# Reordered first stages and cross-attention order, with filler products in TensorE's waits: one core, a chain of twelve small layers

## The chip, the cores and the metric

The kernel runs as one program on one NeuronCore of a Trainium2 chip. Its five instruction streams are TensorE (PE, with its weight loads shown apart as PEld), VectorE (DVE), ScalarE (ACT), GpSimd (POOL) and SyncE (SP), which issues nearly all DMA transfers. The metric is the device time of one execution in microseconds (us); lower is better.

## The reference, cut to what matters

The input x is a sequence of 128 rows of 128 numbers. It passes through twelve layers (four levels, each a cross-attention, a self-attention and a feed-forward part). A context of 2048 rows of 128 numbers is attended to by the cross layers `l0x`, `l1x`, `l2x` and `l3x`. Everything is float32, and each layer needs the whole result of the layer before it.

```python
# l0x (level 0): similarity of each context row and each query, both ways, then one product
S      = sim(norm(x), ctx)                    # [128, 2048]
c2q    = softmax(S, over context) @ ctx       # [128, 128]
q2c    = softmax(max(S, over context)) @ norm(x)      # one row of 128
x      = x + concat(xn, c2q, xn * c2q, xn * q2c) @ W_qv + b_qv
# l0a: linear attention with rotary positions on q and k, projection, residual
# l0f: 16-head attention, router, top 2 of 8 experts, residual
# l1x: 16-head cross-attention over the 2048 context rows, with a mask
# l1a: linear attention;  l1f: four hard-routed trees of 256 leaves (q, k, v, f)
# l2x: 16-head cross-attention over the context;  l2a, l2f: attention, experts
# l3x: 16 heads of width 64 over the context;  l3a, l3f: attention, gated experts
```

The rows' order of dependence is strict: no layer can start its main work before the one before it ends. What does not depend on x (the keys of `l1x`, products of two weight matrices, the relative-distance bias `d.1` to `d.3`, a row that marks masked context rows) can be put anywhere before its use.

## The kernel before

The program is written out by hand: every layer is a function that gives each engine a list of instructions, and each engine works through its list in order. `Steps` is a counting semaphore with names: `plan` fixes the order of the names, `now` marks the instruction that completes one, and `wait_ge(..., at(name))` makes another engine wait for it. So an instruction that waits holds up everything behind it on its own engine.

`l0x` has the start of the program. SP issues twelve loads in one order, the context transposed (`ctxT`, 1 MB) fifth, then `rows` (all row vectors), `ctx`, `w_a` (all weights of level 0 and 1) and `const`. PE runs products of ones as filler, transposes the normalised x, makes four score products of 512 context rows each against `tA`, and DVE takes their maxima. ACT makes the exponentials in four quarters, PE turns each quarter (four transposes, `turn`), DVE or ACT copies it to SBUF and PE weighs the context with it (`weigh`). Only after that comes the short softmax over the row maxima (`l0x.t`, `l0x.row`, `l0x.rowexp`, `l0x.batt`, `l0x.bar`). Then the reciprocal of the sums is spread over a 128x128 tile, turned by a product with the identity (`l0x.rd`), copied, multiplied in, and four products with `w_l0x` and an addition make `l0x.x`.

`l0a` works on x with its norm applied late. Between its own steps it has the keys of `l1x` in four parts of 512 (`keys_tensor` on PE, `keys_scalar` on ACT for the high half, `keys_vector` on DVE for the low half), the mask (`mask.any`, `mask`), and two of three steps of the distance bias. q and k are rotated one after the other by `rotate`, five DVE instructions each. `l0f` starts with `biases_tensor` and its self-attention.

When the last low part is made, SP stacks the keys (`stack_keys`): twelve transfers from SBUF to SBUF and three single-row copies, on the one queue. The first GpSimd instruction of `l1x` waits for all of them, and the norm of `l1x` is behind it.

`cross` is the function of `l1x` and `l2x`. For each of 16 heads it needs the maximum of the scores over the context (`peak`: two score products of 512 on PE, one DVE reduction of 128x1024), and then scores again in the other layout (`score`: one product of 512, into one of three banks), an exponential on ACT and the weighing (`weigh`: four narrow products of 256). The main loop is made of runs: four times peak, score, score; then `turn(q + 1)`, which brings the maxima of the next four heads into the queries (`place` on DVE follows); then eight times `weigh`. DVE takes the sums of four heads at `take`.

`l1f` is the tree stage: gathers of leaves by GpSimd, whose landing PE and DVE wait for. `keep(n, bank)` issues n products of the identity with itself, 128 columns in bfloat16, `keep_wide` the same with 512 columns; neither result is read. `l3x` is the last cross layer; there PE waits for the maxima, DVE and ACT for the first two heads.

## Time and profile before

| | |
|---|---|
| median of 3 runs | 502.78 us (501.64 to 502.9) |
| the profiled execution, its own time | 507.33 us |
| its span, first to last instruction | 505.5 us |
| PE busy | 469.7 us (93%), 4058 instructions |
| DVE busy | 326.9 us (65%) |
| ACT busy | 247.1 us (49%) |
| POOL busy | 69.1 us (14%) |
| mean granted TensorE clock | 0.986 |
| end of `l0x`, `l0a`, `l0f` in the span | 28.07, 38.33, 64.57 us |

The busy shares are averages over stages with different limits, and PE's contains the filler products; a busy PE is not by itself the bound. The stages follow one another strictly, so the end of a stage is the time at which DVE has written the new x, and a stage's length is the distance of two such ends.

### The profile page before, as it was taken

The numbers are of one execution on the slowest core, as the hardware profiler recorded it, in microseconds if no ns is written. First come the engines' busy times: TensorE is split into PE (matmuls) and PEld (weight loads), VectorE is DVE, ScalarE is ACT, GpSimd is POOL, SyncE is SP. The second block draws the span as 40 slices with busy tenths as digits, with TensorE's granted clock in tenths as the row PEclk, the third lists the DMA queues.
The fourth block names the chain that finished last, engine by engine and source line by source line (L and its number), as shares of the span: only waits on it lengthen the run. The fifth ranks groups of instructions, "written<-read, shape, count | busy, mean of one in ns | idle before, by whom it ended". The sixth has DMA issues, their size and how long they took to land.

```text
span 505.5 us, 10078 instructions
## 1 busy us (share of the span) xinstructions
PE 469.7 (93%) x4058; PEld 382.7 (76%) x4058; DVE 326.9 (65%) x802; ACT 247.1 (49%) x490; POOL 69.1 (14%) x152
## 2 busy tenths in 40 slices
PE   8989998999877898999998899889999999999897
PEld 6858885565564786856657789779989989989797
DVE  4676679886645935898526663476777877755544
ACT  6324546777302434666744246356557656522131
POOL 1230134000016120200005015400000000001000
PEclk9999999999998988999999999989999999999999
DMA  7908302900188432100009100000000000029000
GB/s 258 409 6 180 74 1 60 206 10 1 44 315 337 181 109 106 43 1 1 1 10 406 46 1 2 0 1 0 1 1 2 1 1 1 1 80 412 8 1 6
DMA packets 9070, 42.05 MB, mean 83 GB/s; under 512 B 2287, under 2 KB 4919, under 8 KB 6327
## 3 DMA queue, kind: packets, MB, share of 16 engines
q1 hardware_dynamic: 7297, 32.73, 19.9%
q0 software_dynamic: 1728, 8.68, 4.6%
q8 instruction: 32, 0.52, 0.4%
q14 instruction: 13, 0.11, 0.1%
HBM read 34.72 MB, written 0.08 MB: 69 GB/s over the span
## 4 chain that ended last, share of the span: by engine, by line
PE 66%; DVE 18%; issue 6%; ACT 4%; DMA 3%; POOL 2%; POOLq 0%; DVEq 0%; ACTq 0%
PE banks L286 59%; PE banks L289 7%; DVE peaks L1627 4%; DMA region<-in_tree_f,leaf_no 2%; ACT probs L2773 1%; DMA region<-in_tree_q,leaf_no 1%; DVE region L1910 1%; DVE small L2691 1%; DVE nmax L661 1%; ACT probs L689 1%; DVE probs L1910 1%; DVE weights_lo L2701 1%; DVE xnT L409 1%; POOL mv L396 1%; ACT region L1714 1%
## 5 line engine op out<-in xcount | busy, mean ns | idle before, releaser
L1627 DVE TENSOR_REDUCE peaks<-banks 128x1 f32<-128x1024 f32 x56 | 66.2, 1219 | 3.6 <-PE banks L286 2.6
L286 PE MATMUL banks<-identb 128*128 128x128 bf16 x826 | 57.7, 221 | 0.6 <-DVE mv L381 0.6
L286 PEld LDWEIGHTS banks<-identb 128*128 128x128 bf16 x826 | 52.1, 100 | 3.9 <-DVE mv L381 0.9
L2691 DVE TENSOR_REDUCE small<-banks 128x1 f32<-128x1024 f32 x32 | 39.1, 1222 | 21.4 <-PE banks L286 21.1
L2773 ACT ACTIVATE probs<-banks,nmax,rooted 128x1024 f32<-128x1024 f32 x32 | 38.5, 1205 | 24.2 <-DVE nmax L2695 23.6
L2782 ACT CAST weights_hi<-banks 128x512 fp32r<-128x512 f32 x64 | 35.1, 590 | 26.1 <-PE banks L289 23.5
L289 PE MATMUL banks<-p_first,probs 128*128 128x128 f32 x320 | 45.0, 279 | 1.9 <-ACT probs L689 1.1
L2701 DVE TENSOR_TENSOR weights_lo<-banks,weights_hi 128x512 fp32r<-128x512 f32 x64 | 41.5, 683 | 7.6 <-ACT weights_hi L2782 7.6
L1714 ACT ACTIVATE region<-banks,seen 128x512 f32<-128x512 f32 x64 | 37.9, 702 | 12.1 <-PE banks L286 12.0
L289 PEld LDWEIGHTS banks<-p_first,probs 128*128 128x128 f32 x320 | 37.0, 142 | 8.5 <-ACT probs L689 2.5
L1714 ACT ACTIVATE region<-banks 128x512 f32<-128x512 f32 x64 | 33.3, 606 | 16.4 <-PE banks L286 16.0
L396 POOL TENSOR_TENSOR mv<-mv,half 128x1 f32<-128x1 f32 x12 | 6.7, 555 | 236.0 <-DVE mv L390 148.2
L286 PE MATMUL banks<-weights_hi,rows_hi 128*128 128x256 f32 x128 | 37.3, 291 | 0.7 <-DVE weights_lo L2701 0.7
L286 PE MATMUL banks<-weights_lo,rows_hi 128*128 128x256 f32 x128 | 36.2, 283 | 0.0
L286 PE MATMUL banks<-weights_hi,rows_lo 128*128 128x256 f32 x128 | 36.0, 281 | 0.0
L286 PE MATMUL banks<-xnT,region 128*128 128x128 f32 x266 | 33.9, 277 | 0.9 <-DVE xnT L409 0.8
L286 PEld LDWEIGHTS banks<-xnT,region 128*128 128x128 f32 x266 | 31.4, 191 | 1.9 <-DVE xnT L409 1.8
L286 PE MATMUL banks<-region,values 128*32 128x256 f32 x512 | 31.7, 382 | 0.0
L286 PE MATMUL banks<-ctx_hi,query_r 128*128 128x512 f32 x64 | 27.4, 428 | 3.8 <-ACT probs L2773 3.8
L286 PE MATMUL banks<-ctx_hi,query_lo 128*128 128x512 f32 x64 | 25.6, 400 | 0.0
L286 PE MATMUL banks<-ctx_lo,query_r 128*128 128x512 f32 x64 | 25.3, 396 | 0.0
L286 PEld LDWEIGHTS banks<-weights_hi,rows_hi 128*128 128x128 f32 x128 | 24.3, 190 | 0.9 <-DVE weights_lo L2701 0.9
(516 smaller groups left out, 924.3 us busy)
## 6 DMA issues: line engine op xcount, KB each, us to landing
region<-in_w_l2f SPq DMA_DIRECT2D x1, 4096.0 KB, 15.5
region<-in_w_l3f SPq DMA_DIRECT2D x1, 4096.0 KB, 13.4
region<-in_w_b SPq DMA_DIRECT2D x1, 3076.0 KB, 13.6
values<-in_ctx SPq DMA_DIRECT2D x2, 1024.0 KB, 7.6
region<-in_w_l0f SPq DMA_DIRECT2D x1, 2048.0 KB, 21.7
keys_l1x<-shared SPq DMA_DIRECT2D x8, 256.0 KB, 4.0
keys_l2x<-probsT SPq DMA_DIRECT2D x8, 256.0 KB, 4.9
region<-in_w_l3d SPq DMA_DIRECT2D x1, 2048.0 KB, 17.1
```

Source lines behind the costliest of these rows:

```text
L286: return nc.tensor.matmul(o, lhsT, rhs, start=start, stop=stop)
L289: return nc.tensor.transpose(o, i, ident[0:n, 0:n])
L396: nc.gpsimd.tensor_tensor(mv[:, 3:4], mv[:, 2:3], half[:, 0:1], ALU.pow).then_inc(G.sem, G.now(tag + ".rstd"))
L409: nc.vector.tensor_copy(dst[0:n, :], ps[0:n, bank, 0:P]).then_inc(V.sem, V.now(tag + ".T"))
L661: m = nc.vector.tensor_reduce(m4, s, AX.X, ALU.max, negate=True)
L1627: nc.vector.tensor_reduce(peaks[:, h // 4 % 2, i:i + 1], ps[:, 2 * a:2 * a + 2, :], AX.XY, ALU.max, negate=True).then_inc(VM.sem, VM.now(( ...
L1714: nc.scalar.activation(weighed[:, u % HELD * BANK:(u % HELD + 1) * BANK], ps[:, score_bank(u), :], ACT.Exp, scale=seen[:, 0:1] if masked e ...
L1910: m = nc.vector.tensor_tensor_reduce(w, x, w, 1.0, 0.0, ALU.mult, ALU.add, h[:, j:j + 1])
L2691: return nc.vector.tensor_reduce(small[:, half:half + 1], ps[:, 2 * half:2 * half + 2, :], AX.XY, ALU.max)
L2701: nc.vector.tensor_tensor(sides(g, c, weights_lo), turned(g, c).rearrange("p (a b) -> p a b", a=4), sides(g, c, weights_hi).bitcast(F32), ...
L2773: nc.scalar.activation(probs[:, g % 2, o:o + 2 * BANK], ps[:, 2 * half:2 * half + 2, :].rearrange("p a b -> p (a b)"), ACT.Exp, bias=nmax[ ...
L2782: nc.scalar.copy(sides(g, c, weights_hi), turned(g, c).rearrange("p (a b) -> p a b", a=4)).then_inc(A.sem, A.now((tag, "e", g, c)))
```

## The change

In `l0x`: the first memset is that of the ones, and only it is waited for. The loads are in another order and in parts: `ctxT` in four, `rows` in three, `w_a` in two, `const` in two, the mask as a 128x16 tile. The sums of the small row softmax are worked on between the quarters of the large one, the division by the sums is moved into the last instruction, and `l0x.rd` with its spreading, product and copy is gone. Of the two products with `center`, one moves to `l1x`; `d.1` moves to `l0f`. GpSimd prepares its constants while the loads land.

In `l0a`: q and k are rotated together in one set of instructions of twice the width; only two parts of the keys are left, both halves of each are written by ACT (`key_scalar`), and the differences are made by GpSimd in `l0f` (`low_gpsimd`); `biases_tensor` moves here, between the product `l0a.kv` and `l0a.c`.

In `l0f`: the other two parts of the keys, the four differences on GpSimd, `d.1` and `d.2`. In `l1x`: `d.3` and the other product with `center`, ahead of the stage. The three single-row copies of `stack_keys` become four early loads from DRAM.

In `cross`: score goes ahead of peak in each group of three, and `turn` goes into the middle of the eight `weigh`. In `l1f`, `keep` has 60 more products of 128 columns; in `l3x`, 7 and 8 products of 512 columns are put in two waits.

```diff
         def norm_vector(...):
             ...tensor_scalar(mv[:, 2:3], mv[:, 1:2], eps, ...).then_inc(V.sem, V.now(tag + ".var"))
+            if between is not None:
+                between()
             dve.wait_ge(G.sem, G.at(tag + ".rstd"))
@@ sp @@
-            load("ctxT", ctxT[:, :], dram["ctxT"])
-            load("rows", rows_t[:, :], dram["rows"].partition_broadcast(P))
-            load("ctx", values, dram["ctx"])
-            load("w_a", tiles["w_a"][:, :], dram["w_a"])
-            load("const", tiles["const"][:, :], dram["const"])
+            load("mask_by_row", mask_t[:, :], dram["mask"].rearrange("o (p c) -> (o p) c", c=16))
+            for b in QUARTERS:
+                load(f"ctxT{b}", ctxT[:, b * BANK:(b + 1) * BANK], dram["ctxT"][:, b * BANK:(b + 1) * BANK])
+            load_part("rows0", rows_t, dram["rows"], 0, 2, ROWS)
+            load_part("w_a0", tiles["w_a"], dram["w_a"], 0, 5, W_A)
+            load("ctx", values, dram["ctx"])
+            load_part("const0", tiles["const"], dram["const"], 0, 10, CONST)
+            load_part("rows1", rows_t, dram["rows"], 2, 7, ROWS)
+            load_part("w_a", tiles["w_a"], dram["w_a"], 5, len(W_A), W_A)
+            load_part("const", tiles["const"], dram["const"], 10, len(CONST), CONST)
+            load_part("rows", rows_t, dram["rows"], 7, len(ROWS), ROWS)
@@ l0x, pe @@
+                turn(0)
+                turn(1)
+                pe.wait_ge(V.sem, V.at("mask"))
+                product(1, 0, xnT, True, False)
+                weigh(0)
+                pe.wait_ge(V.sem, V.at("l0x.row"))
+                mm(batt, tC[0:1, :], one[0:1, 0:1]).then_inc(T.sem, T.now("l0x.batt"))
+                turn(2)
+                weigh(1)
+                pe.wait_ge(V.sem, V.at("l0x.batt"))
+                mm(bar, xn[:, :], s[:, 8:9]).then_inc(T.sem, T.now("l0x.bar"))
+                turn(3)
+                weigh(2)
+                pe.wait_ge(V.sem, V.at("l0x.f"))
+                product(1, 3, tF, False, True).then_inc(T.sem, T.now("l0x.y0"))
+                weigh(3)
+                fill(6)
+                pe.wait_ge(V.sem, V.at("l0x.prod"))
+                product(2, 2, tE, True, False)
+                pe.wait_ge(V.sem, V.at("l0x.d"))
+                product(2, 1, tD, False, True).then_inc(T.sem, T.now("l0x.y"))
@@ l0x, dve: maxima @@
+                loaded(dve, "rows0")
+                vl(dve, nc.vector.tensor_tensor_reduce(tC[:, :], xn[:, :], at["w1"], ...))
+                nc.vector.tensor_tensor(s[:, 1:2], s[:, 0:1], at["b_sim"], ALU.add)
+                for b in QUARTERS:
+                    dve.wait_ge(T.sem, T.at((tag, "s", b)))
+                    m = nc.vector.tensor_reduce(small[:, b:b + 1], ps[:, b, :], AX.X, ALU.max)
...
+                nc.vector.scalar_tensor_tensor(xs[:, 1 - x_at[tag], :], ps[:, 2, 0:P], s[:, 10:11], xb[:, :], ALU.mult,
+                                               ALU.add).then_inc(V.sem, V.now("l0x.x"))
@@ l0a, pe @@
+                keys_tensor(pe, "l1x", at["w_l1x_k"], 0, 2)
+                keys_tensor(pe, "l1x", at["w_l1x_k"], 1, 3)
+                keep(4, 6)
+                pe.wait_ge(V.sem, V.at("l0a.qk"))
+                mm(ps[:, 1, 0:P], rotated[:, P:2 * P], tC[:, :]).then_inc(T.sem, T.now("l0a.kv"))
+                tr(ps[:, 5, 0:P], rotated[:, 0:P]).then_inc(T.sem, T.now("l0a.q.turned"))
+                pe.wait_ge(G.sem, G.at("wide"))
+                biases_tensor(4)
@@ l0f, pool @@
+                pool.wait_ge(V.sem, V.at("l0f.xn"))
+                for b in range(NB):
+                    low_gpsimd(pool, "l1x", b, shared)
@@ cross, pe @@
                     for i in range(4):
+                        score(RUN * (d + 1) + 2 * i)
                         peak(4 * d + LEAD + i)
-                        score(RUN * (d + 1) + 2 * i)
                         score(RUN * (d + 1) + 2 * i + 1)
...
-                    if c == 0 and q + 1 < QUADS:
-                        turn(q + 1)
                     for u in range(RUN * d, RUN * (d + 1)):
+                        if u == RUN * d + RUN // 2 and c == 0 and q + 1 < QUADS:
+                            turn(q + 1)
                         weigh(u)
@@ l1f, pe: keep() @@
-                keep(8, 0)
+                keep(30, 0)
                 pe.wait_ge(A.sem, A.at("l3x.vo"))
                 tree_tensor(pe, "q")
                 tree_tensor(pe, "k")
+                keep(6, 2)
...
                 first_units(pe, "v")
+                keep(16, 2)
                 pe.wait_ge(A.sem, A.at("l1f.p"))
...
                 tree_tensor(pe, "v")
+                keep(8, 2)
...
-                keep(6, 2)
+                keep(10, 2)
                 turn_tensor(pe, "l1f.y", tB[:, :], "l1f.y", 7)
-                keep(6, 2)
+                keep(10, 2)
@@ l3x, pe @@
                 against_context(1, (0, 1), 1)
+                keep_wide(7, 4)
                 pe.wait_ge(G.sem, G.at("l3x.rows"))
...
+                    if g == 0:
+                        keep_wide(8, 6)
```

## Rows read from the trace of the kernel before

**Rows 1.** Page, part 4: shares of the chain that ended last.

```profile
PE 66%; DVE 18%; issue 6%; ACT 4%; DMA 3%; POOL 2%; POOLq 0%; DVEq 0%; ACTq 0%
```

**Rows 2.** Stretches: start and end, length, busy time (count) by engine, clock, DMA.

```profile
28.10:38.40 10.30, 9.13 (x57) 5.44 (x56) 8.25 (x30) 2.75 (x4) 1.78 (x8) 1.00 0.01 2
82.00:137.00 55.00, 52.12 (x419) 31.78 (x420) 42.99 (x82) 37.91 (x64) 3.45 (x9) 1.00 0.35 69
```

**Rows 3.** DMA issues: KB, us from issue to landing.

```profile
ctxT<-in_ctxT SPq DMA_DIRECT2D x1, 1024.0 KB, 5.5
```

**Rows 4.** Timeline of `l0x`: start, duration, instruction, idle before and releaser.

```profile
2.42 0.43 SPq L312 DMA_DIRECT2D ctxT<-in_ctxT  x1
...
8.04 3.65 PE L286 MATMUL banks<-ctxT,tA 128*128 128x512 f32 x8
...
12.65 0.15 DVE L551 TENSOR_SCALAR nmax<-small 128x1 f32<-128x1 f32 x1
...
16.25 0.63 PE L289 MATMUL banks<-p_first,probs 128*128 128x128 f32 x4
...
16.71 1.06 PE L286 MATMUL banks<-probsT,values 128*128 128x128 f32 x8
...
21.14 0.28 DVE L954 TENSOR_REDUCE small<-banks 1x1 f32<-1x128 f32 x1 [1.95 <-PE banks L289]
...
27.78 0.29 DVE L446 TENSOR_TENSOR xs<-banks,xb 128x128 f32<-128x128 f32 x1 [0.88 <-PE banks L286]
```

**Rows 5.** Timeline of `l0a`, the same columns.

```profile
31.57 0.34 DVE L1090 SCALAR_TENSOR_TENSOR tG<-banks,mv,p_rows 128x128 f32<-128x128 f32 x1
...
34.20 0.49 PE L286 MATMUL banks<-tC,tB 128*128 128x128 f32 x2 [0.42 <-DVE tB L1097]
...
36.46 0.38 PE L286 MATMUL banks<-tE,tD 128*128 128x128 f32 x2
...
37.65 1.14 PE L286 MATMUL banks<-own_bias,sbq 64*128 64x4 f32 x8
...
38.05 0.28 DVE L446 TENSOR_TENSOR xs<-banks,xb 128x128 f32<-128x128 f32 x1
```

**Rows 6.** Timeline: first and last group of 15 key transfers; one GpSimd difference.

```profile
38.16 1.23 SPq L312 DMA_DIRECT2D keys_l1x<-shared  x2
...
52.27 1.25 SPq L312 DMA_DIRECT2D keys_l1x<-keys_l1x  x1
...
72.11 1.28 POOL L1339 TENSOR_TENSOR keysT<-keysT,probsT 128x512 f32<-128x512 f32 x1 [0.86 <-ACT keysT L1333]
```

**Rows 7.** Timeline of `l1x`: two peaks' maxima, then weigh, peak, exponentials.

```profile
102.12 2.35 DVE L1627 TENSOR_REDUCE peaks<-banks 128x1 f32<-128x1024 f32 x2
...
112.47 1.93 PE L286 MATMUL banks<-region,values 128*32 128x256 f32 x32
114.33 0.73 PE L286 MATMUL banks<-keys_l1x,query_r 105*128 105x512 f32 x2
...
115.33 4.74 ACT L1714 ACTIVATE region<-banks,seen 128x512 f32<-128x512 f32 x8 [1.62 <-PE banks L286]
```

**Rows 8.** Stretches of `l1f` and `l3x`, columns as in Rows 2.

```profile
178.00:180.00 2.00, 2.00 (x17) 1.86 (x15) 0.84 (x3) 0.00 (x0) 0.00 (x0) 0.50 0.00 0
...
334.00:336.00 2.00, 2.00 (x11) 1.77 (x10) 0.98 (x1) 1.02 (x4) 0.00 (x0) 0.69 0.00 0
336.00:338.00 2.00, 2.00 (x8) 1.71 (x7) 1.59 (x3) 1.05 (x2) 0.00 (x0) 0.50 0.00 0
```

**Rows 9.** Timeline of PE in `l1f` and `l3x`, columns as in Rows 4.

```profile
156.20 5.73 PE L286 MATMUL banks<-routes,identb 128*128 128x512 bf16 x18 [2.03 <-DMA region<-in_tree_q,leaf_no]
163.36 4.06 PE L286 MATMUL banks<-p_first,region 128*128 128x128 f32 x34 [1.44 <-DVE small L1917]
...
179.46 1.18 PE L286 MATMUL banks<-xnT,shared 128*128 128x128 f32 x4
...
333.29 0.50 PE L286 MATMUL banks<-ctx_hi,query_r 128*128 128x512 f32 x1 [2.05 <-ACT probs L2773]
```

More of the change, by code:

```diff
@@ L250, in build @@
         loads = {n: sem("loaded_" + n) for n in
-                 ("x", "first", "w_k2", "const", "cols", "rows", "w_a", "ctxT", "ctx", "mask", "w_l0f", "l0f_b2", "node",
+                 ("x", "first", "w_k2", "const0", "const", "cols", "rows0", "rows1", "rows", "w_a0", "w_a", "ctxT0", "ctxT1",
+                  "ctxT2", "ctxT3", "ctx", "mask_by_row", "w_l0f", "l0f_b2", "node",
                   *("leaf1_" + t for t in "qkvf"), *("leaf0_" + t for t in "qkvf"),
@@ L312, in load, with load_part @@
             nc.sync.dma_start(dst, src, allow_slow_non_contiguous=scattered).then_inc(loads[name], 16)
+        def load_part(name, tile, source, first, last, pack):
+            at_ = [sum(w for _, w in pack[:i]) for i in range(len(pack) + 1)]
+            c = slice(at_[first], at_[last])
+            if source is dram["rows"]:
+                load(name, tile[:, c], source[c].partition_broadcast(P))
+            else:
+                load(name, tile[:, c], source[:, c])
         def loaded(eng, name):
-            eng.wait_ge(loads[name], {"node": 64, "keys_l1x": 15 * 16, "keys_l2x": 12 * 16}.get(name, 16))
+            eng.wait_ge(loads[name], {"node": 64, "keys_l1x": 16 * 16, "keys_l2x": 12 * 16}.get(name, 16))
         @on("sp")
@@ L869, in l0x @@
-            V.plan("l0x.q", "center")
-            G.plan("prelude", "pairs", "wide")
+            norm_plan(tag)
+            T.plan("l0x.xn.turned")
+            V.plan("l0x.q", "l0x.xn.T", "hidden", "mask.min", "center")
+            G.plan("prelude", "wide", "pairs")
             A.plan(*(("shown", t) for t in range(4)))
-            ctx_plan(tag, 1)
-            V.plan("l0x.t")
-            T.plan("l0x.row")
-            V.plan("l0x.rowmax")
-            A.plan("l0x.rowexp")
-            V.plan("l0x.row")
@@ new lines, in product @@
+                def product(bank, i, f, start, stop):
+                    return mm(ps[:, bank, 0:P], f[:, :], at["w_l0x"][:, i * P:(i + 1) * P], start, stop)
+                pe.wait_ge(G.sem, G.at("one"))
+                fill(30)
+                loaded(pe, "first")
+                turn_tensor(pe, tag + ".xn", xn[:, :], tag + ".xn")
+                fill(8)
+                pe.wait_ge(V.sem, V.at("l0x.q"))
+                for b in QUARTERS:
+                    loaded(pe, f"ctxT{b}")
+                    mm(ps[:, b, :], tA[:, :], ctxT[:, b * BANK:(b + 1) * BANK]).then_inc(T.sem, T.now((tag, "s", b)))
@@ new lines, in _ @@
+                loaded(pe, "w_a0")
+                pe.wait_ge(V.sem, V.at("center"))
+                centred_tensor(pe, 0, 4)
+                mm(ps[:, 7, 400:401], one[:, :], masked_t[:, 16:17]).then_inc(T.sem, T.now("mask.any"))
+                fill(12)
+                pe.wait_ge(V.sem, V.at("l0x.t"))
+                tr(row, s[:, 2:3]).then_inc(T.sem, T.now("l0x.row"))
+                fill(4)
+                turn(0)
+                turn(1)
+                pe.wait_ge(V.sem, V.at("mask"))
@@ L1134, in _ @@
                 loaded(act, "cols")
-                for b in range(NB):
-                    keys_scalar(act, "l1x", at["l1x_bk"], b, 2 + b % 2, shared)
+                key_scalar(act, "l1x", 0, 2, shared, at["l1x_bk"])
+                act.wait_ge(T.sem, T.at("l0a.q.turned"))
+                nc.scalar.copy(tE[:, :], ps[:, 5, 0:P]).then_inc(A.sem, A.now("l0a.q.T"))
+                key_scalar(act, "l1x", 1, 3, shared, at["l1x_bk"])
             @on("pool")
@@ L1163, in _ @@
             def _(pe):
-                pe.wait_ge(G.sem, G.at("wide"))
-                biases_tensor(1)
-                pe.wait_ge(G.sem, G.at("prelude"))
-                keep(14, 0)
+                for b in (2, 3):
+                    pe.wait_ge(A.sem, A.at(("l1x", "k", b - 2)))
+                    keys_tensor(pe, "l1x", at["w_l1x_k"], b, b)
                 pe.wait_ge(V.sem, V.at("l0f.var"))
-                keep(10, 0)
+                keep(6, 0)
                 start_tensor(pe, tag)
```

578 lines of the change are left out of this document (225 added, 353 removed).

## The prediction

> **What bounds the kernel now.** I read the chain of waits first: two thirds of it are PE, a fifth DVE [rows 1], but PE's share contains filler and products that wait in PE's list for DVE. A mean over the span says little here, so I then went through the timeline stage by stage, asking what released each step. The twelve layers are strictly serial: whatever a stage loses is lost, and whatever is off its chain costs nothing.
>
> In `l0x` the score products start at 8.04, when `ctxT` has landed (issued 2.42, 5.5 later, so 7.9), and the maxima are ready at 12.80 (12.65 + 0.15). From there to the new x at 28.07 (27.78 + 0.29) are 15.27 us [rows 3, 4]. The row softmax comes after the whole weighing: its first DVE step is at 21.14 after 1.95 of idle [rows 4]. In `l0a` DVE is busy 8.25 of 10.30 us with things of which the keys, mask and distance are not the stage's own [rows 2]. In the crosses no engine is full (DVE 42.99, ACT 37.91 of 55.00 [rows 2]), so each run is a chain of hand-overs.
>
> **`l0x`: the start.** `ctxT` in quarters lets the first score start when a quarter is there. The quarter is the fifth load as the whole was; I estimate 5.7, between the issue at 2.42 and the whole's 7.9. Four scores take 3.65, so they end at 9.4 rather than 11.7. But DVE now waits for `rows0` ahead of the maxima, and that load is behind all of `ctxT`: not before 7.9, about 8.1, plus 0.6 for the two instructions on it. Four maxima at 0.7 and the two small steps (3.1 together) give 11.7 to 11.9 for the maxima instead of 12.80: I take 11.7, a gain of 1.1. Bounds: nothing if `rows0` is at 9, and 2.3 if `rows0` is no wait.
>
> **`l0x`: after the maxima.** Counted from the maxima (0). ACT: two exponentials of 0.7, the row's exponential 0.5, two more: last at 3.3. PE: a turn is 0.63, a weighing 0.95 (8 passes in 1.06, overlapped) [rows 4]. Turns 0 and 1 end at 2.15; the mask's wait behind DVE's first copy holds PE to 2.5; product 0.25, weighing 0 to 3.7, row product 0.35, turn 2 to 4.7, weighing 1 to 5.6, next row product to 5.9, turn 3 to 6.5, weighing 2 to 7.4, product, weighing 3 to 8.7. Then a DVE product 0.3, another copy behind it, two pairs of passes and the closing instruction: 10.1. Against 15.27 that is 5.2 less. The removed parts are the row softmax behind the weighing (21.14 to about 23.7) and the spreading, product and copies of the reciprocal. `l0x` together gains 6.3; bounds 4.5 (each of six new hand-overs 0.3 worse) and 8.
>
> What leaves `l0x` is hidden later: one product with `center` and `d.3` ahead of `l1x` stand where `keep(16)` stood; DVE's copy of `d.3` (0.41) is in the 0.7 in which it waits for GpSimd's root; `d.1` and `d.2` stand in `l0f`'s waits, where I count 0.1 lost. Without that cover they would cost about 1.5.
>
> **`l0a`.** Both rotations take 31.57 to 34.20, 2.63. At twice the width in one set I work out 1.8: the fixed part of five instructions is saved, the elements are not. The mask and distance steps ahead and between are gone, and so is the fourth key product, behind which the product of 36.46 stood: that came 2.26 after 34.20, with a key difference on DVE between [rows 5]. New chain from x: turned x at 1.0, v and q,k to 1.9, rotated 3.7, `kv` 3.75, turn of q, and then `biases_tensor`, eight small passes, which took 1.14 at 37.65 with nothing waiting, now ahead of `l0a.c`: it starts at 5.3 instead of 4.6. From there the old tail, 38.33 - 36.46 = 1.87. So 7.2 instead of 10.26 [rows 5]: gain 3.1, bounds 2.2 (if ACT's two writes of part 0 hold its copy of q) and 3.7 (if the eight passes are hidden).
>
> **`l0f` and the keys.** The last GpSimd difference decides when SP can stack. GpSimd starts after `l0f.xn`, about 30.6 on the new time; four of 1.28 [rows 6] end at 35.8. The 15 transfers took 38.16 to 53.52; without three of them 11.5, so the last is issued at 47.3 and lands some 4.4 later, 51.7. GpSimd must have them before the norm of `l1x`, at 28.9 + 26.2 + 0.8 = 55.9. The queue has 4 us to spare; I cost it at nothing. The DVE time freed was counted in `l0a`. `l0f` keeps its 26.2, plus the 0.1.
>
> **The crosses.** After weighing ends PE does a peak first (114.33, 0.73 with its tail), and ACT begins only at 115.33 after 1.62 idle; then eight exponentials take 4.74 [rows 7]. Score first brings ACT's start about 0.45 forward. What can take it back is DVE: two maxima take 2.35 [rows 7], a peak may be issued only when the one two before is taken, and `turn` half a weighing later makes `place` 0.95 later. With those limits: the run after a `turn` stays about 6.3 (DVE ends last, no gain), the other falls from 6.67 to about 6.0, also because `turn` no longer waits at the head of the weighing. That is 0.7 to 0.9 per four heads, and 0.3 to 0.45 in the last two runs, where DVE has no peaks. Over three and a half such groups: 2.2 in `l1x`, 1.8 in `l2x` (shorter exponentials, so DVE binds more). Together 4.0; bounds 0 and 5.4 (12 runs by 0.45).
>
> **The filler.** In `l1f` the clock was granted at 0.50, which is 1.2 GHz, in 178 to 180: (1 - 0.5) x 2 = 1.0 us of lost PE time, and the node products there took 1.18 for four passes [rows 8, 9], where others take 0.6. They are on the chain to the last gather. With 24 more fillers just before I take the clock as held: 1.0 gained. Against it, fillers that outlast their wait by 0.1 each, in four places: 0.4. Net 0.6, bounds -1.0 and 1.3. The 22 extra at 154 fill an idle of 2.03 and let the 18 wide ones run at full clock, but nothing waits for these: they end at 160 instead of 161.9. In `l3x` the wait of 2.05 before 333.29 was followed by 0.69 and 0.50 of the clock: 0.62 + 1.0 = 1.6 us lost [rows 8, 9]. Eight wide products at 0.22 are 1.76 and fit in 2.05, seven are 1.54 in the earlier wait of 1.7. I take 1.4, bounds 0 and 1.6.
>
> Sum: 6.3 + 3.1 - 0.1 + 4.0 + 0.6 + 1.4 = 15.3. The profiled execution took 507.33 (span 505.5), so 492.0 in its terms; the median lies 4.55 below it, 502.78 - 15.3 = 487.5.
>
> **The clock and a rule against the change.** The wides now ending at 160 leave PE idle until 163.36: 3.3 us, where 1.44 did no harm and 2.03 (ahead of 156.20) was followed by the half clock [rows 9]. The Trainium skill, "TensorE: Matmul & The Clock Gate", "HAM oscillation", says that waits of PE which are long enough drop the clock and that the work after them starts slow. The longer gap of this change fits that rule; the idle of 2.05 in rows 9 agrees with it. By this the 34 passes of 4.06 after 163.36 would run at half for a while, some 2 us later; DVE sets the chain there and has about 1 us of room, so the loss is up to 1.0: the lower bound above.
>
> The Trainium skill, "DMA: Bandwidth & Descriptors", "Measured", wants transfers of 1 MiB and more, against quarters of `ctxT`. No row here shows a quarter; by the rule the last one and `rows0` come late, which is the rival of the loads below.
>
> **Rivals.** (a) The crosses give nothing: score in front holds the peak back behind ACT's bank, and DVE, 42.99 of 55.00, starves. For it: DVE is the fullest there. Against: DVE idles anyway at every `take`. Gain 15.3 - 4.0 = 11.3, time 491.5; if each of 12 runs loses 0.23, the length of one score, 494. (b) Loads late: the parts land slower than the whole, `rows0` at 10 and `ctx` behind it. Costs 2 to 3 in `l0x`: 490. (c) The fillers hold no clock and the tree's gap drops it: 15.3 - 2.0 - 1.0, time 490.5. (d) Slower than before: the queue of keys. If GpSimd's differences or SP's transfers end late, the norm of `l1x` waits behind them. It begins to cost when the keys land after 55.9, 4.2 later than worked out, and turns the sign only when they land 15.3 + 4.2 = 19.5 later, at 71. That takes 13 us more than the 11.5 for twelve transfers; nothing in rows 6 hints at it. 503 to 506. (e) The change does nothing: the new order only moves the waits. The 5.2 of removed chain in `l0x` speaks against it.
>
> **How the numbers follow.** Main case with its bounds 0.58; (a) 0.17; (b) 0.11; (c) 0.08; (d) 0.03; (e) 0.03. The prediction is the main case, 487.5. All terms at their best give 8 + 3.7 + 5.4 + 1.3 + 1.6 = 20.0, all at their worst 4.5 + 2.2 + 0 - 1.0 + 0 - 0.1 = 5.6, or 482.8 and 497.2. I leave out the ends where all terms would have to agree: 483 to 495, which holds (a) to (c). A difference of 0.3% (1.5 us) is about what a measurement of this kernel can tell from none: faster by more 0.95, within it 0.02, slower by more 0.03.
>
> **What would show it.** `l0x` should end near 21.8, `l0a` 7.2 later, `l0f` 26.2 after that. ACT's first exponential of a run should come 0.6 after the weighing, not 1.0. The windows of 2 us around the end of tree v, and in `l3x` after the second head's exponentials, should show clock 1.00. Keys should be stacked before GpSimd's first instruction in `l1x`. I am wrong if `l0x` ends after 24, if the `cross` runs keep 6.3 and 6.7, or if the clock falls in the tree's new gap and DVE waits for PE there.

## The result and the profile after

| | before | changed |
|---|---|---|
| median, us (lowest to highest) | 502.84 (501.64 to 506.43), 4 runs | 494.69 (493.65 to 496.35), 4 runs |
| ratio of the changed kernel to before | | 0.9835 (95%: 0.9804 to 0.9866) |
| profiled execution, own time / span | 507.33 / 505.5 | 495.39 / 493.6 |
| mean granted clock in it | 0.986 | 0.993 |

The change gains 8.15 us by the medians, where 15.3 was forecast: 494.69 against 487.5. A ratio, here and below, is taken against the kernel before as timed beside that run, whose medians lie between 502.8 and 504.7; so medians of different experiments compare only roughly. By stages (each ends with DVE's write of the new x; us):

| stage | before | before, second profile | changed | gain forecast |
|---|---|---|---|---|
| `l0x` | 28.07 | 28.49 | 24.56 | 6.3 |
| `l0a` | 10.26 | 10.25 | 7.02 | 3.1 |
| `l0f` | 26.24 | 26.24 | 26.25 | -0.1 |
| `l1x` | 71.24 | 71.27 | 70.15 | 2.2 |
| `l1f` | 55.04 | 50.62 | 52.34 | 0.6 |
| `l2x` | 66.00 | 66.18 | 65.19 | 1.8 |
| `l3x` | 139.72 | 137.86 | 138.05 | 1.4 |

The other five stages agree within 0.02 in all three. The column in the middle is an experiment further down; `l1f` and `l3x` cannot be read without it. The stages of the two first profiles differ by 13.0, their spans by only 11.9: from the last write of x to the end of the span, where the output is stored, the changed kernel's profile took 3.1 and the first of before 1.95. All others took 1.9 to 2.0 there, so the 1.1 belongs to that one execution.

The changed kernel's `l0x` in the timeline (start, duration, engine, instruction, idle before it and releaser); its rows answer to [rows 4]:

```profile
4.49 0.43 SPq L315 DMA_DIRECT2D p_rows<-in_rows  x1
4.96 0.43 SPq L315 DMA_DIRECT2D p_w_a<-in_w_a  x1
5.44 0.43 SPq L315 DMA_DIRECT2D values<-in_ctx  x1
5.89 2.82 PE L292 MATMUL banks<-ctxT,tA 128*128 128x512 f32 x6
5.91 1.44 SPq L315 DMA_DIRECT2D p_const<-in_const  x1
7.39 1.51 SPq L315 DMA_DIRECT2D p_rows<-in_rows  x1
...
9.07 1.12 PE L292 MATMUL banks<-ctxT,tA 128*128 128x512 f32 x2 [0.36 <-DMA ctxT<-in_ctxT]
...
10.97 0.29 DVE L850 CUSTOM_DVE_ANT_0 tC<-xn,p_rows 128x128 f32<-128x128 f32 x1 [4.77 <-DMA p_rows<-in_rows]
...
11.38 2.48 DVE L856 TENSOR_REDUCE small<-banks 128x1 f32<-128x512 f32 x4
...
12.24 1.55 PE L292 MATMUL banks<-p_w_a,center 128*128 128x384 f32 x2 [2.05 <-DMA p_w_a<-in_w_a]
...
14.09 0.15 DVE L859 TENSOR_SCALAR nmax<-small 128x1 f32<-128x1 f32 x1
...
24.21 0.35 DVE L895 SCALAR_TENSOR_TENSOR xs<-banks,small,xb 128x128 f32<-128x128 f32 x1 [0.60 <-PE banks L292]
```

The first three scores follow one another without a wait, but DVE stands for 4.77 us before its first use of `rows0`, and then takes four maxima in a row that could have gone between the scores. The maximum is ready at 14.24, which is 1.4 later than before, not 1.1 earlier. From there to the end it is 10.32 instead of 15.27; that half of the change works. PE idles meanwhile, from 10.19 to 12.24, and then the granted clock falls to 0.50, which is 1.2 instead of 2.4 GHz (the same kernel by stretches, columns as in [rows 2]):

```profile
10.00:12.00 2.00, 0.19 (x1) 0.00 (x0) 0.99 (x5) 0.00 (x0) 0.00 (x0) 1.00 1.03 420
12.00:14.00 2.00, 1.76 (x6) 1.15 (x7) 1.97 (x5) 0.00 (x0) 0.00 (x0) 0.59 0.97 404
14.00:16.00 2.00, 2.00 (x21) 1.94 (x19) 0.55 (x4) 1.57 (x5) 0.10 (x1) 0.55 1.07 433
```

`l0a`, against [rows 5]: the eight small passes start at 28.91, and `l0a.c` (the product of `tE` and `tD`) follows them.

```profile
28.91 0.29 DVE L1042 SCALAR_TENSOR_TENSOR tD<-banks,p_const 128x128 f32<-128x128 f32 x1 [0.58 <-PE banks L292]
28.91 1.14 PE L292 MATMUL banks<-own_bias,sbq 64*128 64x4 f32 x8
29.02 0.27 ACT L1053 COPY tE<-banks 128x128 f32<-128x128 f32 x1 [0.30 <-PE banks L295]
29.91 0.47 PE L292 MATMUL banks<-tE,tD 128*128 128x128 f32 x2
...
31.29 0.29 DVE L471 TENSOR_TENSOR xs<-banks,xb 128x128 f32<-128x128 f32 x1 [0.58 <-PE banks L292]
```

A pair of runs in `l1x`, against [rows 7]: in the first run (98.44) `turn` is inside the weighing, which is thus split, and ACT starts 2.62 after the weighing's start; in the second 2.39. Before it was 2.86 (115.33 - 112.47).

```profile
98.44 1.28 PE L292 MATMUL banks<-region,values 128*32 128x256 f32 x19
99.55 1.05 PE L292 MATMUL banks<-region,values 128*32 128x256 f32 x13
...
101.06 4.86 ACT L1635 ACTIVATE region<-banks,seen 128x512 f32<-128x512 f32 x8 [1.54 <-PE banks L292]
104.94 1.94 PE L292 MATMUL banks<-region,values 128*32 128x256 f32 x32
107.33 4.28 ACT L1635 ACTIVATE region<-banks,seen 128x512 f32<-128x512 f32 x7 [1.42 <-PE banks L292]
```

`l1f` around the new gap behind the wide fillers (they end at 152.29, PE goes on at 154.78), by stretches:

```profile
153.00:155.00 2.00, 0.22 (x2) 0.22 (x3) 1.59 (x4) 1.19 (x5) 1.20 (x2) 1.00 1.04 422
155.00:157.00 2.00, 1.83 (x13) 1.74 (x13) 1.98 (x18) 1.25 (x5) 0.00 (x0) 0.68 1.01 424
157.00:159.00 2.00, 2.00 (x11) 2.00 (x11) 1.93 (x18) 0.00 (x0) 0.00 (x0) 0.50 1.00 405
```

The low stretch did come right behind that gap, as was feared. Those of [rows 8] are gone, but they were gone in the second profile of before too.

### The profile page after: what moved, and what is told of

Same layout as the page of the kernel before. It is cut to its first block, busy times and chain, and to the rows that moved or that the text cites. A ratio compares the mean times of both kernels' runs of the same rounds, so it can differ in the third digit from the quotient of the medians.

```text
span 493.6 us, 9957 instructions
## 1 busy us (share of the span) xinstructions
PE 463.6 (94%) x3994; PEld 375.7 (76%) x3994; DVE 317.9 (64%) x789; ACT 249.8 (51%) x494; POOL 73.9 (15%) x156
## 4 chain that ended last, share of the span: by engine, by line
PE 67%; DVE 12%; issue 7%; DMA 5%; ACT 4%; POOL 3%; SPq 1%; POOLq 0%; DVEq 0%; ACTq 0%
PE banks L292 60%; PE banks L295 7%; DMA region<-in_tree_v,leaf_no 2%; DVE peaks L1546 2%; DMA region<-in_tree_f,leaf_no 2%; DMA p_w_a<-in_w_a 1%; ACT probs L2700 1%; DVE small L2618 1%; POOL region L1748 1%; POOL mv L421 1%; DVE nmax L557 1%; SPq L315 1%; ACT probs L585 1%; DVE weights_lo L2628 1%; DVE xnT L434 1%
## 5 line engine op out<-in xcount | busy, mean ns | idle before, releaser
L1635 ACT ACTIVATE region<-banks,seen 128x512 f32<-128x512 f32 x64 | 38.3, 700 | 10.5 <-PE banks L292 10.3
L292 PEld LDWEIGHTS banks<-region,values 128*32 128x32 f32 x512 | 16.2, 109 | 13.4 <-ACT region L1635 2.9
```

Source lines behind the costliest of these rows:

```text
L292: return nc.tensor.matmul(o, lhsT, rhs, start=start, stop=stop)
L1635: nc.scalar.activation(weighed[:, u % HELD * BANK:(u % HELD + 1) * BANK], ps[:, score_bank(u), :], ACT.Exp, scale=seen[:, 0:1] if masked e ...
```

## The experiments

Twelve runs: eleven kernels, and the kernel before once more. Unless a text says otherwise, "the changed kernel" is their base.

**rows_first**

```diff
+            load_part("rows0", rows_t, dram["rows"], 0, 2, ROWS)
             for b in QUARTERS:
                 load(f"ctxT{b}", ...)
-            load_part("rows0", rows_t, dram["rows"], 0, 2, ROWS)
```

> The changed kernel with one issue moved: the load of the first two row vectors (`rows0`) is issued ahead of the four quarters of `ctxT`, not behind them. Theory: DVE waits at the head of the maxima only for this load; in the changed kernel it landed at 10.97 though the fourth score ended at about 10.2 and the first at 6.7. With it first it lands by 7 to 8, DVE takes the maxima as the scores come, and the last quarter, one issue (0.43) later, sets them: scores end at 10.6, maxima ready at about 11.7 to 12.0 instead of 14.24, l0x 2.2 to 2.5 us shorter, and nothing after it changes. Rival: the queue gives the transfers a fixed share, so the broadcast row load delays the quarters by as much as it took, the last quarter lands at 10 or later, and l0x gains 1 us or less.

Median 491.55, ratio 0.9785 (0.9748 to 0.9821), which overlaps the changed kernel's 0.9804 to 0.9866 a little. `l0x` 21.95, 2.61 shorter, of which 0.5 is the clock, which did not fall here; `l0a`, `l0f` and both crosses as in the changed kernel. Timeline:

```profile
6.12 0.29 DVE L850 CUSTOM_DVE_ANT_0 tC<-xn,p_rows 128x128 f32<-128x128 f32 x1
...
8.00 0.69 DVE L856 TENSOR_REDUCE small<-banks 128x1 f32<-128x512 f32 x1 [1.38 <-PE banks L292]
...
9.87 1.13 PE L292 MATMUL banks<-ctxT,tA 128*128 128x512 f32 x2 [0.19 <-DMA ctxT<-in_ctxT]
...
11.03 0.69 DVE L856 TENSOR_REDUCE small<-banks 128x1 f32<-128x512 f32 x1 [0.63 <-PE banks L292]
...
11.95 0.15 DVE L859 TENSOR_SCALAR nmax<-small 128x1 f32<-128x1 f32 x1
```

The maxima now follow the scores; the last quarter sets the end. Maximum at 12.10, end 9.85 later. What the two orders do to the queue is seen in the DMA view (0 to 16 us in 40 slices, GB/s; then KB and us from issue to landing), first of the changed kernel:

```profile
GB/s 0 0 0 0 78 113 156 61 19 175 261 256 302 271 271 379 328 225 129 32 26 42 128 196 225 352 437 420 461 430 410 438 387 416 368 432 423 436 428 447
ctxT<-in_ctxT SPq DMA_DIRECT2D x4, 256.0 KB, 3.7
p_rows<-in_rows SPq DMA_DIRECT2D x1, 64.5 KB, 6.5
```

and of rows_first:

```profile
GB/s 0 0 0 0 108 99 116 74 31 41 53 116 86 268 375 353 369 353 266 302 215 102 230 333 420 461 471 410 410 426 384 404 387 405 415 452 411 457 291 382
ctxT<-in_ctxT SPq DMA_DIRECT2D x4, 256.0 KB, 4.0
p_rows<-in_rows SPq DMA_DIRECT2D x1, 64.5 KB, 3.5
```

With `rows0` in the middle there is a trough of 26 to 42 GB/s from 7.6 to 8.8, and SP's issues there take 1.44 and 1.51 instead of 0.43; with it in front the low rates (31 to 116) come from 2.8 to 5.2, and no single issue takes over 0.74. The price is that the first score starts at 6.86 instead of 5.89; it costs nothing at the end, because the last quarter sets that.

**dot_after**

```diff
-                loaded(dve, "rows0")
-                ...tensor_tensor_reduce(tC, xn, at["w1"], ...); tensor_tensor(s[:, 1:2], ...)
                 ... four maxima, the maximum of them ...
                 nc.vector.tensor_scalar(nmax[:, 0:1], small[:, 4:5], -1.0, ...)
+                loaded(dve, "rows0")
+                ...tensor_tensor_reduce(tC, xn, at["w1"], ...); tensor_tensor(s[:, 1:2], ...)
```

> The changed kernel with the loads as they are, but DVE's wait for `rows0` and its two instructions moved behind the negated maximum, so that the maxima wait for the scores alone. Theory: the maxima follow the scores (three are there by 8.6, the fourth at about 10.2), so the maximum is ready at about 11.2 instead of 14.24, and the exponentials start 3 us earlier; the row's path then starts behind `rows0` (10.97, plus 0.6), still ahead of the first copy. l0x 2.5 to 3 us shorter. Rival: the chain then hangs on the load of w_a0, which lands at 12.2 and stands in PE's list ahead of the turns, so that l0x gains only about 1 to 1.5.

Median 493.04, ratio 0.9811 (0.9773 to 0.985); `l0x` 23.97. The maximum is ready at 12.91, so 1.3 earlier than in the changed kernel, not 3: the score passes came 0.85 apart at first (6.99, 7.84, 8.70, 9.55) and 0.43 only at the end (10.78, 11.21), though the granted clock of these stretches reads 1.00. And from the maximum to the end it was 11.06, not 9.7 to 9.9 as elsewhere at clock 1.00: the products that wait for `w_a0` (13.28) stand in PE's list ahead of the row's product (14.84), and ACT's third exponential stands behind the row's (15.46). So `l0x` gained 0.59 on the changed kernel's profile, less than the rival's 1 to 1.5, by two causes; on the mean of the five profiles with this order of loads and of DVE's work, 25.5 (below), it is 1.5.

**ctx_whole** (base: rows_first)

```diff
-            for b in QUARTERS:
-                load(f"ctxT{b}", ...)
+            load("ctxT0", ctxT[:, :], dram["ctxT"])
```

> The kernel of rows_first (row vectors issued first), but with ctxT again as one transfer of 1 MiB, which the four scores wait for. Theory: the quarters gain because the first scores start early, but the last quarter landed as late as 9.9 (issue of the first at 3.06, so 6.8 later), where the whole took 5.5 in the kernel before. If small pieces are what is slow, the whole lands at about 8.5 and the four scores end at about 12.2, the maxima are ready at 13.3, l0x 1.3 longer than with rows_first (21.95). Rival: what is slow is the company of the loads issued behind; then the whole lands no earlier than the last quarter did, at 9.9, the scores end at 13.5, and l0x is 2.5 to 3 longer.

Median 495.51, ratio 0.9838 (0.9778 to 0.9898); `l0x` 27.35. Timeline:

```profile
9.82 6.70 PE L292 MATMUL banks<-ctxT,tA 128*128 128x512 f32 x8 [3.97 <-DMA ctxT<-in_ctxT]
```

The whole is there at 9.82, the last quarter in rows_first was at 9.87, in one execution of each: nothing here says that the pieces made it late. The quarters start the work 3 us earlier. Of the 5.4 that `l0x` lost, 3.05 are the scores themselves (6.70 instead of 3.65 [rows 4], clock 0.50 from 10 to 15); the rest, 2.35, is just under the rival's 2.5 to 3.

**held_back** (base: rows_first)

```diff
             for b in QUARTERS:
                 load(f"ctxT{b}", ...)
+            loaded(sp, "ctxT3")
             load_part("w_a0", ...)
```

> The kernel of rows_first, in which SP issues the loads behind ctxT (w_a0, ctx and all the rest) only when the last quarter of ctxT has landed. Theory: the last quarter is late (9.9 in rows_first, 10.6 in others, 5.4 to 6.2 after its issue, where the first three are ready by 8) because the megabytes issued behind it share the engines with it. Alone, 1.1 MB at the 350 to 450 GB/s that the loads reach later take 3 us from about 5, so the last quarter is there by 8, the scores end at 8.9 and the maxima at 10.3 instead of 12.1; w_a0 then comes at about 11 to 12 and ctx at 13, just when the first weighing wants it: l0x ends at 20 to 21 instead of 21.95. Rival: the last quarter is late by itself, at the rate of the queue in these first microseconds (100 to 350 GB/s); then it lands no earlier, everything behind it comes 3 to 5 us later, the weighing waits for ctx, and l0x ends at 25 or later.

Median 493.23, ratio 0.9808 (0.9776 to 0.984); `l0x` 23.23. SP could issue `w_a0` at 8.84:

```profile
8.84 0.33 SPq L315 DMA_DIRECT2D p_w_a<-in_w_a  x1
```

So the last quarter was there 1.0 before rows_first's 9.87. That fits the theory that the loads behind it delay it, but it is one execution of each, and the last quarter of unchanged orders varied by 1.5 (9.07 to 10.61), so it is not shown. And the clock was low just then, so the scores ended at 12.33:

```profile
7.00:9.00 2.00, 2.00 (x3) 0.97 (x4) 0.09 (x1) 2.00 (x2) 1.72 (x7) 0.53 0.53 197
9.00:11.00 2.00, 2.00 (x4) 0.73 (x4) 0.99 (x2) 0.32 (x1) 0.27 (x2) 0.62 0.57 106
```

`w_a0`, which was expected at 11 to 12, came at 12.54. Neither the theory's end of `l0x` nor the rival's came: `l0x` is 1.3 longer than in rows_first.

**spread_biases** (base: rows_first)

```diff
@@ l0a, pe @@
-                biases_tensor(4)
                 ... l0a.c ...
-                keep(8, 7)
+                biases_tensor(1, (0, 1))
@@ l0f, pe @@
-                pe.wait_ge(V.sem, V.at("l0f.var"))
-                keep(6, 0)
+                biases_tensor(1, (2, 3))
                 start_tensor(pe, tag)
```

DVE's three copies of the results move behind the turned xn in `l0f`.

> The kernel of rows_first with the eight small passes of biases_tensor taken from ahead of l0a.c: four stand behind it, where fillers were, and four in l0f where PE waits for the root. Theory: these passes cost 0.6 in the chain of l0a, as predicted; l0a is 0.6 shorter (6.4 instead of 7.02), less 0.25 by which four of them outlast DVE's copy, and l0f stays at 26.25. Rival: q's copy by ACT, which ended at 26.68, sets l0a.c, and the passes that move into l0f make the turn of xn late: l0a gains 0.3 and l0f loses as much.

`l0a` 6.60 (7.02), `l0f` 26.25: 0.42 for nothing, near the theory's 0.35. `l0x` was 23.94: the clock fell at 8 (0.65 and 0.50 in the two stretches from 8 to 12), and the first quarter came at 7.74 instead of 6.86; rows_first, with the same order there, kept the clock. Timed once: 491.05.

**cross_old, score_only, turn_only**: the edits of [rows 7]'s loop undone together, or one alone kept.

```diff
 cross_old and turn_only:
-                        score(RUN * (d + 1) + 2 * i)
                         peak(4 * d + LEAD + i)
+                        score(RUN * (d + 1) + 2 * i)
 cross_old and score_only:
+                    if c == 0 and q + 1 < QUADS:
+                        turn(q + 1)
                     for u in range(RUN * d, RUN * (d + 1)):
-                        if u == RUN * d + RUN // 2 and c == 0 and q + 1 < QUADS:
-                            turn(q + 1)
                         weigh(u)
```

> The changed kernel with both edits to PE's order in the crosses undone (peak ahead of the first score of a run, turn ahead of the whole weighing). Theory: l1x is longer by 1.1 and l2x by 0.8, as the stages were before, so the time is about 1.9 us above the changed kernel's and the 4.0 that were predicted for these edits are too much by half. Rival: the edits gave more and something else of the change (the two steps moved ahead of l1x) took a part of it back: then both crosses get longer by more than the 1.1 and 0.8.

> The changed kernel with the score ahead of the peak as changed, but turn ahead of the whole weighing again. Theory: both edits were priced by one sum, with the score as the larger part: l1x keeps 0.8 of its gain of 1.1 to 1.25 and l2x 0.6 of 0.8. Rival: the score in front alone brings nothing, since DVE ends these runs last, and it is turn's later place that frees the exponentials: then l1x and l2x are at 71.4 and 66.0, as with both undone.

> The changed kernel with turn in the middle of the weighing as changed, but the peak ahead of the first score of each pair again. Theory: l1x keeps about 0.3 and l2x 0.2 of their gains. Rival: the whole gain is here, l1x at 70.15 and l2x at 65.2.

| | `l1x` | `l2x` | from weighing to weighing in `l1x`, first four | ACT's wait for scores in `l1x` |
|---|---|---|---|---|
| before | 71.24 | 66.00 | 6.52, 6.63, 6.40, 6.35 | 12.0 |
| cross_old | 71.38 | 65.98 | 6.51, 6.63, 6.40, 6.36 | 12.1 |
| score_only | 70.87 | 66.33 | 6.33, 6.85, 6.21, 6.10 | 11.1 |
| turn_only | 71.36 | 66.15 | 6.72, 6.36, 6.72, 6.35 | 12.0 |
| changed | 70.15 | 65.19 | 6.49, 6.18, 6.50, 6.00 | 10.3 |

The last column is in the view of the waits, first of cross_old and then of the changed kernel (instruction waited for, us, times, longest):

```profile
ACT region L1635 <- PE banks L292: 12.1, 7, 2.4
```

```profile
ACT region L1635 <- PE banks L292: 10.3, 7, 2.4
```

Undoing both brings the old stages back, so the two edits are the whole gain, 1.2 in `l1x` and 0.8 in `l2x`. Cross_old's median (494.50, ratio 0.9836, 0.98 to 0.9871) does not show these 2.0: its interval alone is 3.6 us wide, and stages that wait for DRAM vary by 2. The stages of the crosses, which repeat within 0.2, do. Both single expectations missed: the first two runs sum to 13.15 before, 13.18 with the score alone, 13.08 with `turn` alone and 12.67 with both. Over `l1x` and `l2x` together, cross_old has 137.36, the score alone 137.20, `turn` alone 137.51 and both 135.34. The score alone gains 0.5 in `l1x` and loses 0.35 in `l2x` (66.33 against 65.98), so they only pay as a pair. Timed once each: 498.23 and 497.62.

**fill_old**: the fillers' counts in `l1f` as before (8, 0, 10, 0, 0, 6, 6) and no wide ones in `l3x`.

```diff
-                keep(30, 0)
+                keep(8, 0)
-                keep(16, 2)
...
-                keep_wide(7, 4)
...
-                        keep_wide(8, 6)
```

> The changed kernel without the fillers that it adds: in l1f the counts are 8, 0, 10, 0, 0, 6, 6 again, and the 15 wide ones of l3x are gone. Theory: l1f 2.7 longer with two stretches at half clock (around 178 to 181 and 195 to 200 of the kernel before), l3x 1.7 longer with a fall to 0.5 to 0.7 after the second head's exponentials; together 4.4 us. Rival: the low stretches of the kernel before were chance in one profiled execution that was slow; then the fillers are worth 1.0 to 2.5 and the clock stays at 1.00 in one or both places without them.

**before_again**: the kernel before, unchanged, profiled once more.

> The kernel before, profiled a second time. Theory: l1f of its first profile, 55.04, holds two falls of the clock (178 and 195) that are chance: a second execution shows another pattern and an l1f of 51 to 53, since the changed kernel without its fillers had 50.61 and no fall. The fall in l3x at 335 comes again, and l3x is 139.7 again. Rival: the falls belong to the order of the kernel before; then l1f is 55 and the falls stand in the same places.

Fill_old's median is 493.25, ratio 0.9794 (0.9748 to 0.9839), no worse than the changed kernel's. Its `l1f` is 50.61 with the clock at 1.00 throughout, shorter than the changed kernel's 52.34; but other profiles with the fillers go down to 50.12. Its `l3x` is 139.61 with a fall. Before_again took 501.71 (its own time), with `l1f` 50.62 and `l3x` 137.86 and no fall in either. What this says of `l3x` is in PE's rows there, of fill_old:

```profile
322.28 0.50 PE L292 MATMUL banks<-ctx_hi,query_r 128*128 128x512 f32 x1 [2.05 <-ACT probs L2694]
```

and of before_again:

```profile
329.50 0.50 PE L286 MATMUL banks<-ctx_hi,query_r 128*128 128x512 f32 x1 [2.05 <-ACT probs L2773]
```

and in the stretches behind them, of fill_old:

```profile
323.00:325.00 2.00, 2.00 (x10) 1.62 (x9) 0.64 (x1) 0.89 (x3) 0.00 (x0) 0.59 0.00 0
325.00:327.00 2.00, 2.00 (x9) 1.76 (x8) 1.59 (x3) 1.17 (x2) 0.00 (x0) 0.55 0.00 0
```

and of before_again:

```profile
329.00:331.00 2.00, 1.50 (x7) 1.21 (x8) 0.31 (x1) 2.00 (x5) 0.00 (x0) 1.00 0.00 0
331.00:333.00 2.00, 2.00 (x14) 1.80 (x13) 1.82 (x3) 1.18 (x3) 0.00 (x0) 1.00 0.00 0
```

The same product, the same wait of 2.05 ahead of it as in [rows 9], and once the clock falls and once it does not. So a low stretch is not settled by the order of the instructions: it comes in one execution and not in another.

**combined** and **combined_held** (base: spread_biases)

```diff
                 pe.wait_ge(V.sem, V.at("l0x.q"))
+                fill(18)
                 for b in QUARTERS:
+                    if b == 3:
+                        fill(8)
@@ l1f: fillers as before; combined_held also: @@
             load_part("w_a0", ...)
+            loaded(sp, "ctxT3")
             load("ctx", values, dram["ctx"])
```

> The changed kernel with what the runs so far point to: row vectors issued first, the eight small passes split (four behind l0a.c, four in l0f), 18 fillers in PE's wait for the first quarter of ctxT and 8 ahead of the last one, and the fillers that the change added to l1f taken out again (those of l3x stay). Theory: the clock holds through the scores, so that l0x ends at 21.9 (rows_first, where the clock held by itself) and not at 23.9 (spread_biases, where it fell at 8); l0a is 6.6; l1f is 50 to 51 without a fall, as in both profiles that had no added fillers and no fall. Median 489 to 490.5 against rows_first's 491.5. Rival: the fillers do not hold the clock while only a load is waited for, l0x is 22 to 24 as it falls, and the median is 491 or more; or the low stretch in l1f comes back near 157, as in the first profile of before.

> The kernel of combined, in which SP issues the load of ctx and those behind it only when the last quarter of ctxT has landed (w_a0 stays ahead of it). Theory: held_back had the last quarter at 8.8 instead of 9.9 and lost it to the clock, which fell at 7, and to w_a0, which came at 12.5. With the clock held and w_a0 earlier the scores end at 10, the maxima are ready at about 11, and l0x ends at 21 or a little below, 0.5 to 1 better than combined. Rival: w_a0's 512 KB are company enough to keep the last quarter late, and ctx, 3 us later than in combined, holds the first weighing: l0x 22 to 23, no better than combined or worse.

| | median | ratio | `l0x` | maximum ready | `l0a` | `l1f` |
|---|---|---|---|---|---|---|
| combined | 491.80 | 0.9736 (0.9704 to 0.9768) | 22.70 | 12.98 | 6.62 | 52.16 |
| combined_held | 491.93 | 0.9738 (0.9706 to 0.977) | 22.62 | 12.90 | 6.60 | 52.41 |

The clock read 1.00 through both `l0x`, as the theory had it; rows_first shows that it can also hold without fillers, so two profiles don't prove that the fillers held it. The medians missed 489 to 490.5: the first quarter came late in both (7.67 and 7.59, 6.86 in rows_first); the eight fillers in front of the last score (10.35) were a delay of some 0.4 in combined_held, where the last quarter was there before 9.61; and the low stretch at the wide fillers of `l1f` came back in combined (0.87 and 0.50 from 145 to 149), as in the first profile of before. Holding the loads back brought nothing with `w_a0` still ahead: the last quarter was there at 9.6, not 8.8. Both versions beat the changed kernel: their intervals do not meet its 0.9804 to 0.9866. That they beat rows_first is not shown: its median is 491.55, and its interval, 0.9748 to 0.9821, overlaps both of theirs.

## Why the prediction was off by half of the gain

**`l0x`, the start: this step failed.** The prediction put `rows0` at 8.1, "behind all of `ctxT`: not before 7.9", and the last quarter at the landing time of the old whole. In the five profiles with this order of loads and of DVE's instructions (after, cross_old, fill_old, score_only, turn_only) DVE began with it at 10.97, 11.29, 12.35, 11.88 and 11.50, always 1.3 to 1.9 after the last score could start (9.07 to 10.61). So the order of the queue was read rightly, and the landing times wrongly: 7.9 is the landing of the whole in the old queue, and was taken over for a new one. What in the new queue makes the last quarter later was not isolated. With `rows0` in front the forecast start is there (12.10 against 11.7) and `l0x` ends at 21.95 against 21.8. This is the rival (b), "loads late", whose 10 for `rows0` was still too early; the own mark "wrong if `l0x` ends after 24" was met by 24.56. Its reason, that the parts land slower than the whole, finds no support: in ctx_whole the whole took 6.6 from issue to landing, and in rows_first four quarters in the same place were complete at the same time (9.87 against 9.82). The Trainium skill, "DMA: Bandwidth & Descriptors", "Measured", gives 6.15 us for 1 MB issued from GpSimd, counted while the DMA engines are busy with it; issued from SP and counted from issue to landing it was 5.5 and 5.0 in the two profiles of before and 6.6 in ctx_whole.

**A clock fall in `l0x` was not in the prediction.** It fell in four of the five profiles of that order (not in cross_old). The time from the maximum to the end was 9.72 to 9.85 in the seven profiles in which the clock was at 1.00 by then (cross_old, rows_first, spread_biases, held_back, ctx_whole and both combined ones), and 10.32 to 11.24 in after, fill_old, score_only and turn_only, where it was not; dot_after has another order there. Forecast was 10.1: right where the clock holds, and 0.5 to 1.5 us are lost where it does not. The mean `l0x` of the five is 25.5, a gain of 2.8 on 28.3 where 6.3 stood: 3.5 of the missing 7.15.

**`l0a`: right.** 7.02 against 7.2, and the 0.6 named for `biases_tensor`: 0.42 came back when it was spread.

**`l0f` and the keys: right.** 26.25, and GpSimd's root ahead of `l1x` waits for DVE's `mv` and for no key. The keys landed at 55.4, not 51.7, but the norm is later too, and GpSimd idles 2.76 after them; the slower case (d) did not come. (In its sum, 19.5 later would have taken 19.5 us more than the 11.5 for the transfers, not 13.)

**The crosses: the mechanism right, the term of 4.0 twice too large.** It gave 2.0. Forecast were 0.7 to 0.9 for each pair of runs; the first two pairs gained 0.48 and 0.25 (6.52 + 6.63 to 6.49 + 6.18, and 6.40 + 6.35 to 6.50 + 6.00). The exponentials do come early: 0.45 after the weighing's end (107.33 - 106.88), where 0.6 was forecast and the kernel before had 0.93. So the wait that the edits were to shorten did get shorter, and the step that failed is what a run gains by it: the run that holds `turn` gains 0.03 and then loses 0.10, the other gains 0.45 and 0.35. The prediction named DVE as what can take it back and said that no engine is full; it left out PE, which [rows 2] shows busy 52.12 of 55.00, and which is about as busy in the like window after:

```profile
74.00:129.00 55.00, 51.96 (x422) 31.20 (x421) 44.20 (x84) 38.67 (x65) 4.25 (x11) 1.00 0.34 67
```

DVE has 44.20 here and had 42.99 [rows 2]. That the fullness of PE halved the term is only argued, since busy time of PE contains the modelled ends of its products; no run tests it. Why the pair needs both edits is not shown by any row here, only that it does. (The prediction's own rate, 0.7 to 0.9 over three and a half groups, would even have been 2.45 to 3.15 for `l1x`, not 2.2.)

**The fillers: this step failed too.** The terms of 0.6 and 1.4 were read off falls in one profile, and then subtracted from a median that lay 4.55 below that profile. Before_again has none of them and took 501.71, so the four falls of the first profile are not the kernel's rule. But an execution near the median is not free of falls: a profile with none has a mean clock of 1.000, one with one short fall (about 4 us) 0.996 or 0.997, one with two such 0.993, the first of before with four 0.986. Of the seven executions of before that were timed beside before_again, five read 0.992 or 0.993 and took 503.22 to 504.35, and two read 0.997 and 0.999 and took 502.21 and 502.45. The four of the changed kernel read 0.992 to 0.997. So most executions of either kernel lose something to the clock, some 1 us for a fall by these times (an estimate); where, no trace of them says. In `l3x` it fell in 2 of 3 profiles without the wide fillers and in 0 of 11 with them. So they do hold it, for 1.6 where it falls (139.7 against 138.1) and -0.1 to -0.4 where it does not. In `l1f` nothing is shown for the 60 narrow ones: `l1f` is 50.12 to 52.34 in the nine profiles with them (mean 51.4) and 50.61, 50.62, 52.16, 52.41 and 55.04 in the five without. Six of the nine have a low stretch around the end of the gap behind the wide ones. The idle before PE goes on was 1.88 to 3.37 in these six and 2.48 to 2.97 in the three without a fall, and 2.05 in all three cases in `l3x`, of which one had no fall: its length does not tell the two apart. The Trainium skill, "TensorE: Matmul & The Clock Gate", "HAM oscillation", was cited for that gap: that long waits of PE drop the clock fits the six, and not the other three. The longer gap was to cost up to 1.0; `l1f` is 51.6 in the mean of the six and 51.0 in that of the three, which is less than either group varies. Falls and gathers from DRAM are mixed there, and I cannot part them. That stays open.

Together: 3.5 (`l0x`) + 2.0 (crosses) are 5.5 of the missing 7.15, and the fillers' 2.0 cover the rest. Counted from the other side, 2.8 (`l0x`) + 3.2 (`l0a`) + 2.0 (crosses) are 8.0 of the measured 8.15, which leaves next to nothing for the fillers in the median. This sum takes `l0x` from seven profiles and the 8.15 from eight timed executions, so it fits, and proves no more. That 494.69 lies inside 483 to 495 is partly luck: it is 0.3 from the edge, and none of the rivals (a) to (c) gives it alone (the worst form of (a) comes nearest, 494). Half of (a), all of (b) and most of (c) came together. The first two profiles differed by 11.9 rather than 8.15 because the one of before held three falls of the clock in `l1f` and one in `l3x`; before_again, without any, is 6.3 longer in its span than the changed kernel's profile with two.

## What to carry to other kernels

Here a load in four pieces was complete as soon as the whole, but the wait that mattered moved to the smallest thing behind it: put the few kilobytes that the first engine needs in front, and do not let an engine wait for them ahead of work that doesn't use them. Before costing a clock fall, profile the same kernel twice; a term read from an execution that lies above the median may not be subtracted from the median. Two reorderings of one loop can be worth next to nothing singly (0.2 and -0.2 over two stages) and 2 us together, so undo them one at a time as well as both. Before writing that no engine is full, look at PE too.

## What the runs showed that I had not expected

- A row broadcast to 128 partitions (64.5 KB) took 6.5 to 7.8 us from issue behind 1 MiB and 3.5 to 4.4 in front of it. With it in the middle, single issues on SP took up to 2.99 instead of 0.43. That it is this transfer's small pieces (516 bytes for each partition) which stall the queue is only argued.
- Score passes came 0.85 apart in dot_after from 7 to 9.6, twice the usual 0.43, while the granted clock of these stretches reads 1.00. There the pace of the passes tells more than that column.
- `l1a`, `l2a`, `l2f`, `l3a` and `l3f` repeat within 0.02 us over 14 profiles; `l0x` and `l1f`, which wait for DRAM and hold most of the clock's falls, vary by 2 us in the same order of instructions, and with them every small comparison of whole times.
